# Twelve-layer kernel on one core: maxima of the first context attention on GpSimd, a bias load moved, a film-and-filter section in two stages, gelu by columns

## What is computed

```python
sim = jnp.einsum('hid,hjd->hij', qh, kh) * SCALE
mean = jnp.mean(sim, axis=-1, keepdims=True)
sim = (sim - mean) * ATTN_MATRIX_SCALE + mean
attn = jax.nn.softmax(sim, axis=-1)
out = jnp.einsum('hij,hjd->hid', attn, vh)
...
return jnp.einsum('bni,iq->bnq', out, Wout) + bout
```

```python
c_t = c_t * text_mask[..., None]
x = layernorm(x_text, g_norm_in, b_norm_in)
scale_in, shift_in = jnp.split(c_t @ W_film_in + b_film_in, 2, axis=-1)
x = x * (1.0 + mod_gate * scale_in) + mod_gate * shift_in
y = s4d(x, log_dt, A_re, A_im, C_re, C_im, D_skip)
scale_out, shift_out = jnp.split(c_t @ W_film_out + b_film_out, 2, axis=-1)
y = y * (1.0 + mod_gate * scale_out) + mod_gate * shift_out
xt = x_text + y
h = layernorm(xt, g_ffn, b_ffn)
h = jax.nn.gelu(h @ W1 + b1, approximate=False) @ W2 + b2
```

## Time and profile before

| | |
|---|---|
| median of 3 runs | 4770.83 us (4765.56 to 4775.98) |
| profiled execution, its own time | 4773.13 us |
| its span in the trace | 4771.4 us |
| PE busy, share of span | 3660.8 us, 77% |
| DVE | 3005.6 us, 63% |
| ACT | 1894.5 us, 40% |
| POOL | 260.7 us, 5% |
| first context attention (L956), about | 224 to 1727 us |
| layer 2, mask to last addition | 3561.1 to 3634.3 us |

### The profile page before, as it was taken

One profiled execution on the slowest core, in us unless ns is written; L12 is line 12 of the kernel. 1 busy time (PEld: TensorE's weight loads), 2 busy tenths in 40 slices (PEclk: granted clock), 3 DMA queues, 4 the chain that ended last, 5 costly groups with the idle time before them and its releaser, 6 DMA issues. The chain is left out here.

```text
span 4771.4 us, 54706 instructions
## 1 busy us (share of the span) xinstructions
PE 3660.8 (77%) x21928; PEld 1970.9 (41%) x21928; DVE 3005.6 (63%) x4214; ACT 1894.5 (40%) x2113; POOL 260.7 (5%) x112
## 2 busy tenths in 40 slices
PE   4699999999999955577776772666544785879669
PEld 2434444444444423233336552332222464545356
DVE  3466666666666666589885437699985446442541
ACT  1255555555555532244441332244431343331123
POOL 0000000000000000000000000144430000000000
PEclk9799999999999977799997895666656986888789
DMA  2000000000000000100002001000001000000000
GB/s 74 8 0 0 1 0 0 0 1 0 0 1 0 1 11 12 20 8 7 8 1 85 27 2 38 0 0 0 0 0 37 2 36 8 36 1 0 1 10 32
DMA packets 12879, 55.80 MB, mean 12 GB/s; under 512 B 2209, under 2 KB 2721, under 8 KB 11970
## 3 DMA queue, kind: packets, MB, share of 16 engines
q1 hardware_dynamic: 12626, 52.31, 3.7%
HBM read 48.50 MB, written 0.52 MB: 10 GB/s over the span
## 5 line engine op out<-in xcount | busy, mean ns | idle before, releaser
L985 PE MATMUL banks<-L0x_q_context,L0x_context 96*128 96x512 f32 (+1 forms) x1632 | 742.0, 596 | 10.0 <-ACT L0x_ring L1079 9.3
L1010 PE MATMUL banks<-L0x_ring,L0x_context_rows 128*97 128x512 f32 (+1 forms) x1632 | 737.5, 594 | 1.1 <-ACT L0x_ring L1065 1.1
L1079 ACT COPY L0x_ring<-banks 128x1024 f32<-128x1024 f32 (+1 forms) x416 | 413.4, 996 | 657.8 <-PE banks L985 657.8
L1129 DVE TENSOR_TENSOR L0x_maxima<-L0x_maxima,L0x_ring 128x1024 f32<-128x1024 f32 (+1 forms) x288 | 342.6, 1194 | 257.2 <-ACT L0x_ring L1079 256.1
L1110 DVE TENSOR_TENSOR L0x_ring<-L0x_ring,L0x_spread 128x2048 f32<-128x2048 f32 (+1 forms) x208 | 457.2, 2200 | 18.4 <-ACT L0x_spread L1053 18.4
L985 PEld LDWEIGHTS banks<-L0x_q_context,L0x_context 96*128 96x128 f32 (+1 forms) x1632 | 300.1, 188 | 396.7 <-issue 378.0
L1010 PEld LDWEIGHTS banks<-L0x_ring,L0x_context_rows 128*97 128x97 f32 (+1 forms) x1632 | 262.0, 164 | 416.8 <-issue 413.6
L1065 ACT ACTIVATE L0x_ring<-L0x_ring 128x2048 f32<-128x2048 f32 (+1 forms) x208 | 384.4, 1849 | 11.4 <-DVE L0x_ring L1110 11.3
L1485 ACT ACTIVATE L1x_probs<-banks 128x2048 f32<-128x2048 f32 (+1 forms) x112 | 196.7, 1757 | 260.3 <-PE banks L1415 218.5
L1518 DVE TENSOR_REDUCE L1x_maxima<-banks 128x3 f32<-128x1203 f32 (+1 forms) x176 | 241.5, 1372 | 91.2 <-PE banks L1384 91.2
L1384 PE MATMUL banks<-L1x_k,L1x_q 32*128 32x401 f32 x1024 | 181.3, 591 | 120.3 <-DVE L1x_maxima L1518 104.8
(11 more groups left out here) (899 smaller groups left out, 5512.4 us busy)
## 6 DMA issues: line engine op xcount, KB each, us to landing
L1f_expert_weights<-in_L1f_experts SPq DMA_DIRECT2D x16, 512.0 KB, 10.9
L2f_expert_weights<-in_L2f_experts SPq DMA_DIRECT2D x8, 512.0 KB, 5.0
L3a_expert_weights<-in_L3a_experts SPq DMA_DIRECT2D x8, 512.0 KB, 5.1
L3f_expert_weights<-in_L3f_experts SPq DMA_DIRECT2D x8, 512.0 KB, 5.7
L1x_k<-L1x_k_rows SPq DMA_DIRECT2D x64, 50.0 KB
L0x_context_rows<-in_context_rows SPq DMA_DIRECT2D x1, 2448.0 KB, 27.8
L0x_context<-in_context SPq DMA_DIRECT2D x1, 2401.5 KB, 19.4
L1x_context<-in_context SPq DMA_DIRECT2D x4, 600.4 KB, 5.1
```

The costliest lines, as they stand in the source:

```text
L985: mm = pe.matmul(k.ps[0:height(j), i, :], c1[:, j * P:j * P + height(j)], q1[:, u // 2 % 2, :], start=True, stop=True)
L1010: mm = pe.matmul(k.ps[0:CW, bank, :], rows1[0:height(j), j, :], ring[0:height(j), s % RING, i, :], start=s == FIRST[u] and i == 0, stop=s ...
L1079: act.copy(ring[0:r, s % RING, 2 * p:2 * p + len(pair), :], k.ps[0:r, 2 * p:2 * p + len(pair), :]).then_inc(copied, 1)
L1129: dve.tensor_tensor(o, before, ring[0:r, s % RING, 2 * p:2 * p + m, :], ALU.max).then_inc(maxed, 1)
```

## The change

1. `attend_all_places`: `turn`, `spread_out`, `greatest` and `place` are gone. `fold(u)` signals `folded`; for odd u it first takes the maximum with the even unit's result. GpSimd does `partition_all_reduce` of 128 x 512 to `greatest`, and DVE subtracts it.
2. `ContextAhead.load`: the output bias is issued second and no longer last.
3. Layer 1's flag goes over the partitions by a product with ones on PE, not by GpSimd.
4. Layer 2: the mask is loaded with the filter's tables; mask, normalisation, transposes and both film products are one stage, `steer`; the filter, the output film and the addition are a second, `filter_long`. The gate is multiplied into the film weights and biases once. The spectra are read from the banks and not copied, and the products are started in fours.
5. Gelu: eight ACT operations read the banks as the products end; no DVE share, no separate pass.

```diff

-            def turn(u):
-                pe.wait_ge(folded, u + 1)
-                if u:
-                    pe.wait_ge(placed, u)
-                for a in range(4):
-                    mm = pe.transpose(k.ps[:, 6, a * P:(a + 1) * P], folded_top[:, a * P:(a + 1) * P], k.ident[:])
-                mm.then_inc(turned, 1)
-
-            def spread_out(u):
-                pe.wait_ge(negated, u + 1)
-                for a in range(4):
-                    mm = pe.transpose(k.ps[:, 6, a * P:(a + 1) * P], neg[:, u % 4, a:a + 1].broadcast_to([P, P]), k.ident[:])
-                mm.then_inc(spread, 1)
...
         def _(act):
-            def place(u):
-                act.wait_ge(spread, u + 1)
-                if u >= 2:
-                    act.wait_ge(shifted, LAST[u - 2] + 1)
-                    act.wait_ge(differed, u // 2)
-                act.copy(spread_top[:, u % 2, :], k.ps[:, 6, :]).then_inc(placed, 1)
...
                 dve.wait_ge(half_fold, u + 1)
-                dve.tensor_tensor(folded_top[:], top[:, 0, 0, :], top[:, 0, 1, :], ALU.max).then_inc(folded, 1)
-
-            def greatest(u):
-                dve.wait_ge(turned, u + 1)
-                ins = dve.tensor_reduce(neg[:, u % 4, :], k.ps[:, 6, :].rearrange("p (a j) -> p a j", a=4), X, ALU.max, negate=True)
+                if u:
+                    dve.wait_ge(placed, u)
+                ins = dve.tensor_tensor(folded_top[:], top[:, 0, 0, :], top[:, 0, 1, :], ALU.max)
                 if u % 2:
-                    ins.then_inc(reduced, 1)
-                    dve.wait_ge(reduced, u // 2 + 1)
-                    dve.wait_ge(negated, u)
-                    ins = dve.tensor_tensor(neg[:, u % 4, :], neg[:, u % 4, :], neg[:, u % 4 - 1, :], ALU.min)
-                ins.then_inc(negated, 1)
+                    ins.then_inc(joined, 1)
+                    dve.wait_ge(joined, u // 2 + 1)
+                    ins = dve.tensor_tensor(folded_top[:], folded_top[:], greatest[:, 0, :], ALU.max)
+                ins.then_inc(folded, 1)
...
+        @block.gpsimd
+        def _(pool):
+            for u in range(UNITS):
+                pool.wait_ge(folded, u + 1)
+                if u >= 2:
+                    pool.wait_ge(shifted, LAST[u - 2] + 1)
+                    pool.wait_ge(differed, u // 2)
+                pool.partition_all_reduce(greatest[:, u % 2, :], folded_top[:], P, RMAX).then_inc(placed, 1)
...
     def load(self, k, sp):
         self.begun = True
         sp.dma_start(self.heads[:], k.dram["L0x_heads"]).then_inc(self.here, 16)
+        sp.dma_start(self.bout[:], k.dram["L0_xattn_rows"].broadcast_to([P, P])).then_inc(self.here, 16)
         sp.dma_start(self.c1[:].rearrange("c (b n) -> c b n", b=B), k.dram["context"].rearrange("b c n -> c b n")).then_inc(self.here, 16)
         sp.dma_start(self.rows1[:, :, 0:CD], k.dram["context_rows"]).then_inc(self.here, 16)
-        sp.dma_start(self.bout[:], k.dram["L0_xattn_rows"].broadcast_to([P, P])).then_inc(self.here, 16)
...
             def _(pe):
+                pe.wait_ge(counted, 1)
+                pe.matmul(k.ps[:, 1, 0:1], k.ones[:], flag[:, 0:1], start=True, stop=True).then_inc(everywhere, 1)
                 pe.wait_ge(widened, 1)
                 for b in range(B):
                     mm = pe.matmul(k.ps[:, 0, b * P:(b + 1) * P], c_wide[:, b, :], w["v"], start=True, stop=True)
                 mm.then_inc(product, 1)
-
-            @block.gpsimd
-            def _(pool):
-                pool.wait_ge(counted, 1)
-                pool.partition_all_reduce(flag[:, 1:2], flag[:, 0:1], P, RMAX).then_inc(everywhere, 1)
...
                 dve.wait_ge(everywhere, 1)
+                step(dve.tensor_copy(flag[:, 1:2], k.ps[:, 1, 0:1]))
                 step(dve.tensor_copy(mask.rearrange("p t n -> p (t n)"), flag[:, 1:2].broadcast_to([P, TILES * H * d])))
...
+            @block.tensor
+            def _(pe):
+                pe.wait_ge(masked, 1)
+                for t in range(TILES):
+                    pe.transpose(k.ps[:, t // 4, t % 4 * P:(t % 4 + 1) * P], ct[:, t, :], k.ident[:]).then_inc(turned, 1)
+                pe.wait_ge(gated, 2)
+                for t in range(0, TILES, 2):
+                    pe.wait_ge(moved, t // 4 + 1)
+                    for i in range(2):
+                        mm = pe.matmul(k.ps[:, 2 + t // 2, i * 2 * P:(i + 1) * 2 * P], cT[:, (t + i) * P:(t + i + 1) * P], w["film_in"],
+                                       start=True, stop=True)
+                    mm.then_inc(product, 1)
+                for t in range(0, TILES, 2):
+                    for i in range(2):
+                        mm = pe.matmul(k.ps[:, (6 + t // 2) % 8, i * 2 * P:(i + 1) * 2 * P], cT[:, (t + i) * P:(t + i + 1) * P], w["film_out"],
...
+                dve.tensor_tensor(ct[:], ct[:], mask[:, :, None].broadcast_to([P, TILES, P]), ALU.mult).then_inc(masked, 1)
+                for n in names:
+                    dve.tensor_scalar(w[n], w[n], w["gate"], None, ALU.mult).then_inc(gated, 1)
+                for i, n in enumerate(names):
+                    step.start(dve.tensor_scalar(shift[:, i, :], w["b_" + n], w["gate"], None, ALU.mult))
+                step.settle()
+                step(dve.tensor_scalar(shift[:, :, 0:P], shift[:, :, 0:P], 1.0, None, ALU.add))
...
+                for p in range(4):
+                    dve.wait_ge(product, p + 1)
+                    step.start(dve.tensor_tensor(film[:, 0, 2 * p:2 * p + 2, :], k.ps[:, 2 + p, :].rearrange("p (t n) -> p t n", t=2),
+                                                 shift[:, 0, None, :].broadcast_to([P, 2, 2 * P]), ALU.add))
+                step.settle()
+                step(dve.tensor_tensor(xin[:], xin[:], film[:, 0, :, 0:P], ALU.mult))
+                dve.tensor_tensor(xin[:], xin[:], film[:, 0, :, P:2 * P], ALU.add)
...
+                pe.wait_ge(free, 4)
+                for f in range(2):
+                    pe.wait_ge(ready, f + 1)
+                    for i in range(TPB):
+                        for part in range(2):
+                            table = w["sin_f" if part else "cos_f"]
+                            mm = pe.matmul(k.ps[:, i, :], table[:, f * S + i * P:f * S + (i + 1) * P],
+                                           ys[:, part, f].rearrange("p b d -> p (b d)"), start=f == 0 and part == 0, stop=f == 1 and part == 1)
+                        if f == 1:
+                            mm.then_inc(back, 1)
...
+                for p in range(4):
+                    dve.tensor_tensor(film[:, 1, 2 * p:2 * p + 2, :], k.ps[:, (6 + p) % 8, :].rearrange("p (t n) -> p t n", t=2),
+                                      shift[:, 1, None, :].broadcast_to([P, 2, 2 * P]), ALU.add).then_inc(free, 1)
+                for f in range(2):
...
+                    step.start(dve.tensor_tensor(ys[:, 0, f], real, kc, ALU.mult))
+                    step.start(dve.tensor_tensor(tmp[:, 0], imag, ks, ALU.mult))
+                    step.start(dve.tensor_tensor(ys[:, 1, f], real, ks, ALU.mult))
+                    step.start(dve.tensor_tensor(tmp[:, 1], imag, kc, ALU.mult))
+                    step.settle()
+                    step.start(dve.tensor_tensor(ys[:, 0, f], ys[:, 0, f], tmp[:, 0], ALU.subtract))
+                    step(dve.tensor_tensor(ys[:, 1, f], ys[:, 1, f], tmp[:, 1], ALU.add))
+                    dve.sem_inc(ready, 1)
+                step(dve.tensor_tensor(xin[:], xin[:], w["D_skip"][:, None, :].broadcast_to([P, TILES, P]), ALU.mult))
+                scales, shifts, rows, outs = (by_time(a) for a in (film[:, 1, :, 0:P], film[:, 1, :, P:2 * P], z0, xt))
+                dve.wait_ge(free, 4)
+                for i in range(TPB):
+                    dve.wait_ge(back, i + 1)
+                    step(dve.tensor_tensor(times[:, i], times[:, i], k.ps[:, i, :].rearrange("p (b d) -> p b d", b=B), ALU.add))
+                    step(dve.tensor_tensor(times[:, i], times[:, i], scales[:, i], ALU.mult))
+                    step(dve.tensor_tensor(times[:, i], times[:, i], shifts[:, i], ALU.add))
+                    dve.tensor_tensor(outs[:, i], times[:, i], rows[:, i], ALU.add)
...
+        @block.scalar
+        def _(act):
+            for n, (f, half) in enumerate(items):
+                act.wait_ge(product, n + 1)
+                act.activation(h[:, f, half * 512:(half + 1) * 512], k.ps[:, n, :], ACT.Gelu, bias=bias[:, f:f + 1])
...
-            def modulate(target, bias):
-
-                def write(dve, step, t, product):
-                    step(dve.tensor_tensor(film[:], product, bias, ALU.add))
-                    step(dve.tensor_scalar(film[:], film[:], w["gate"], None, ALU.mult))
-                    step(dve.scalar_tensor_tensor(out=target[:, t, :], in0=film[:, 0:P], scalar=1.0, in1=target[:, t, :], op0=ALU.add, op1=ALU.mult))
-                    step(dve.tensor_tensor(target[:, t, :], target[:, t, :], film[:, P:2 * P], ALU.add))
-                return write
```

(12 more changed lines are left out.)

157 lines of the change are left out of this document (81 added, 76 removed).

## The result

The changed kernel took 4683.65 us (median of 4 runs, 4679.35 to 4689.03) against 4768.87 for the kernel before (4 runs, 4765.56 to 4775.98). The ratio is 0.982, with a 95% interval of 0.9802 to 0.9838: faster by 77 to 94 us. The forecast was 4676, with 4660 to 4706 as its range. The profiled execution took 4679.6 us, with a span of 4677.9; in the profiled pair the spans differ by 4771.4 - 4677.9 = 93.5 us.

What follows compares the result with a forecast made beforehand. PE was taken to bound the first context attention, busy 1488.8 of 1503 us. Gains of 23.8 + 27.5 + 0 + 4.5 + 34 + 5.7 = 95.5 us from the profiled 4773.1 gave 4677.6, 4675.3 against the median; forecast 4676, range 4660 to 4706.

Steps and rivals of the forecast that it cites:

- The start: First loads: the bias's issue waits behind 6528 short rows; issuing it second gains 23.8 us, bounds 0 and 24.2.
- Rival 1: Start: the 24 us aren't recovered, as SP's end of stage or the fourth issue takes them; 4700 us, chance 8%.
- Transposes: First context attention: 0.44 + 0.44 us of PE saved per unit, 28.2 in 32 units, 27.5 after some is hidden.
- GpSimd: First context attention: each 128 x 512 reduction takes 0.5 to 11.0 us, hidden beside PE, so it costs nothing.
- The estimate of 62 us: GpSimd reduction by another operation's documented figure, a quarter of 247.7 us; 32 would make a loss of about 400 us.
- The deadline: Odd units of the first attention: 11.1 us from the joining maximum until the first shift needs GpSimd's result.
- Rival 2: Attention: reductions hold DVE from two-operand SBUF work; 4.4 us free, then up to 32 us per microsecond; chance 8%.
- Rival 3: Attention: maxima come late; reductions over 11.1 us delay the shift, past 15.5 us PE waits; chance 3%.
- rival 4: Attention: PE's gaps fill again with waits for copies, so the 27.5 us don't come; 4704 us, chance 5%.
- Flag: Layer 1's flag: a product with ones replaces DVE's 5.63 us wait for POOL; gain 4.5 us, bounds 3.5 and 5.0.
- Layer 2: Two stages, `steer` 17.1 us and `filter_long` 22.4, replace seven taking 73.2; gain taken as 34 us.
- Gelu: Gelu section: table load, pass and one meeting go, and the next products may run at a higher clock; 5.7 us.

Runs made afterwards that it cites:

- the two orders of issues: Changed kernel with the output bias issued third, 4679.66 us; changed kernel with the context's short rows third and long rows last, 4696.82 us (one run each).
- four reductions: Changed kernel with every GpSimd reduction made four times in a row: 4688.69 us, ratio 0.9814 to the kernel before.
- the first comparison: Changed kernel against the kernel before, four runs each: 4683.65 us against 4768.87, ratio 0.982.
- the second: Changed kernel measured again, unchanged, against the kernel before: 4678.17 us (5 runs) against 4780.57 (9 runs), ratio 0.9788.
- the parts alone: Four kernels, each the kernel before with one part: bias issued second 0.9942; GpSimd maxima 0.9921; layer 2 stages 0.9931; flag and gelu 0.9988.
- in the second: Kernel before with only GpSimd's reduction of the first context attention's maxima (item 1): 4736.1 us, ratio 0.9921.
- in the fourth: Kernel before with only layer 1's flag by a product with ones and the gelu from the banks: 4770.37 us, ratio 0.9988.
- the kernel with one first stage: Changed kernel with its first stages joined and the context issued right behind the weights: 4668.98 us, ratio 0.9768 to the kernel before.

## Why the prediction was right, step by step

*The start.* Forecast 23.8, measured 23.5. Rival 1 is out by the issue times. The reason given, the transfer of many short rows and neither the number of issues nor the bytes, is shown by the two orders of issues. What the prediction didn't say is that the wait also holds the time of what stands ahead of the short rows (14.27 against 24.20), and that it ends before the short rows have landed.

*Transposes.* Forecast 27.5, read 25.5 in the profiled pair. The term was sized too low, not too high: from first maximum to last addition kernels that began the stage in the same way differ by 1490.8 - 1462.4 = 28.4 us, or 1489.50 - 1461.48 = 28.0, the 28.2 of 32 units. The 0.7 us held back for the first ten steps weren't lost. The profiled pair shows less, since the kernel before began its attention in the quicker way and the changed one in the slower (14.05 and 15.6 us), and the same holds for the last products (some 1 us).

*GpSimd.* The bounds were 0.5 and 11.0 us; alone it is 1.80 us, beside VectorE's work 3.75 to 4.35. (1.80 - 0.49) / 505 is 2.6 ns a column: the line of 21 ns was far too steep. The estimate of 62 us, a quarter of the Trainium skill's figure for another operation (GPSIMD Engine Reference, 3.2 Cross-partition), would have been 14 times too much here or more; no run shows that operation itself. The deadline, worked out at 11.1 us, is 11.5 in the traces, and it is borne out: four reductions, 11.5 us, just fit. It holds for 15 of the 16 odd units. In the last one the prediction overlooked that the steps are shorter: the room is 5.2 us, so its upper bound of 11.0 was not "just hidden" there. By the difference, an estimate, it would have cost some 6 us once; four reductions cost 4.9. Rival 2 had a real mechanism: subtractions of 3.14 us for 2.28, and reductions longer by the operation they met. The Trainium skill (SBUF — State Buffer, SBUF: two separate sides) has it as a lock for a whole instruction; VectorE's delay here was 0.86 us of a reduction of 1.78. As 4.4 us were free, it priced at nothing. Rival 3 stays out for the same lengths, rival 4 by TensorE's 1462.70 us busy of 1478.5.

*Flag.* Forecast 4.5, measured 4.8, and the term's reason is only half right. VectorE did wait for GpSimd, but the prediction gave the gain to the product with ones. In the kernel with item 1 alone the wait is gone as well (0.51 us for 5.63), so item 1 would have gained it in the changed kernel too, and item 3 on top of it costs 0.3 us (2.54 against 2.24). The prediction read that GpSimd's operation is made ready within these 5.6 us, but not that it would then already be ready at the flag. The sum holds all the same, since it counts these microseconds once; which edit brings them it had wrong. The wait behind the cast is 0.18 us, not 0.5.

*Layer 2.* Forecast 34, measured 34.8: `steer` 17.1 in the forecast and 16.5 in the trace (3505.10 to 3521.62), `filter_long` 22.4 and 21.9 (to 3543.48).

*Gelu.* Forecast 5.7, measured 6.3: 4.9 up to the first of the products behind it (23.6 and 18.8 us from the last addition) and 1.4 on them, which took 7.38 us at a granted clock of 1.00 where they took 8.77 at 0.84. ScalarE's last pass ends at 3561.94 and the next products start at 3562.23, 0.3 us behind, as forecast.

*The sum.* 95.5 forecast and 94.9 in the edited stretches. Against the medians the forecast was 93.5 and the first comparison says 77 to 94, the second 95 to 109 (0.9773 to 0.9802 of 4780.57). That the parts alone add up to more (27.7 + 37.7 + 33.0 + 5.7 = 104 by their ratios) is in part a double count, since the flag's 5 us are in the second and in the fourth; the rest is within their intervals. Where the medians' 8 us against the profiled pair come from can be named but not divided: the unedited stretch ahead of the attention is 178.0 us in one profile of the changed kernel and 183.3 in the other (199.26 - 15.97), and between the attention's last addition and the flag's reduction, which no edit touches, thirteen profiles show 775.8 to 784.9 us.

## What to carry to other kernels

Where one engine is busy 99% of a stage, an operation taken off it is worth its full length, and the engine that gets the work costs nothing until its result is late; work out that point for the last unit too, then double the work to test it. An issue that takes microseconds is a queue that waits: look for the transfer with many short rows ahead of it, and put that last. A sum of parts is best checked stretch by stretch between equal operations, since stretches with the same code move by 5 us and more here, more than some parts are worth. And before a gain is given to an edit, look at the traces of the single edits: two of them can remove the same wait, as items 1 and 3 do here.

## What the runs showed of the hardware beyond that

- GpSimd's reduction over the partitions of 128 x 512 takes 1.80 us alone, 3.75 and 4.35 beside a VectorE operation of 2.28 us with both operands in SBUF. That operation took 3.14 when the reduction had begun 0.04 us ahead of it, and its plain 2.28 when the reduction had begun 0.43 us ahead.
- A DMA issue behind a transfer of 6528 short rows took 14.27 us, and 24.20 with 2.4 MB more in front; it ended 6.0 and 6.2 us behind the landing of what stood ahead of the short rows. Behind 2.4 MB of long rows it took 0.47.
- GpSimd's first reduction over the partitions started 5.2 us behind its operand (the flag of the kernel before, behind selects, copies and memsets); with such reductions in the attention, and only copies and memsets since, it started 0.1 us behind it.
- The same folding products ran at 0.42 us from pair to pair or at 0.80, in two executions of one program: TensorE's granted clock was 1.00 (the 2.4 GHz level) there in the one, and 0.55, near the 1.2 GHz level, in the other. No edit did that.
- GpSimd's first select came 9.45 us behind its memsets, and 12.65 in the kernel with one first stage, with the context's loads (2448 and 2401.5 KB among them) beside it.
